# A kernel of cross-attention and sixteen routed experts: sorted places given out two batches at a time, on GpSimd, into tiles left open; two groups of 26 and 6 batches instead of three

## What is computed

```python
# attention: 16 heads of 64, softmax(q k^T + mask) v, then Wo
x = x + xattn(layernorm(x), ctx, ctx, mask, Wq, Wk, Wv, Wo, 16)
# experts: 16 of inner width 128, the 4 best of each token, and one shared by all
scores = sigmoid(xt @ gate_w.T); _, idx = top_k(scores + gate_b, 4)
w = 2.5 * w / sum(w)
for e in range(16): y = y + c_e[:, None] * (silu_and_mul(xt @ w13_e.T) @ w2_e.T)
x = x + y + silu_and_mul(xt @ w13_s.T) @ w2_s.T
```

## Time and profile before

| | us |
|---|---|
| median of 3 runs (lowest, highest) | 2112.61 (2112.27, 2116.42) |
| span of the profiled execution | 2199.6 |
| attention phase in it, to PE's first unit | 1562.3 |
| expert phase in it | 637.3 |

### The profile page before, as it was taken

How to read it: one execution, slowest core, us unless ns; L and a number is a source line. 1 busy time by engine, 2 the same in 40 slices (tenths; PEclk the granted TensorE clock), 3 DMA queues, 4 the chain that set the end, 5 groups by cost and what they waited for, 6 DMA issues and landing times. The chain is left out here.

```text
span 2199.6 us, 57839 instructions
## 1 busy us (share of the span) xinstructions
PE 2073.7 (94%) x16404; PEld 1991.0 (91%) x16404; DVE 1873.9 (85%) x6177; ACT 1681.9 (76%) x4795; POOL 1399.5 (64%) x2094
## 2 busy tenths in 40 slices
PE   7999999999999999999999999999799998898885
PEld 6999999999999998999999998999799898887884
DVE  7999999999999999999999999999864446666687
ACT  6998989889988988988888888889755554454441
POOL 4565655555555555778788877877656646656665
PEclk9999999999999999999999999999999999999997
DMA  7777877778777777866666666666678778888897
GB/s 206 183 184 182 195 182 190 179 179 191 189 185 187 183 171 175 214 181 173 176 179 173 176 168 172 171 173 178 218 263 272 266 244 283 272 285 268 271 335 243
DMA packets 262128, 457.32 MB, mean 208 GB/s; under 512 B 36544, under 2 KB 148672, under 8 KB 261824
## 3 DMA queue, kind: packets, MB, share of 16 engines
q1 hardware_dynamic: 237248, 386.48, 65.4%
q0 software_dynamic: 24576, 67.14, 9.6%
HBM read 141.00 MB, written 144.70 MB: 130 GB/s over the span
## 5 line engine op out<-in xcount | busy, mean ns | idle before, releaser
L812 POOL TENSOR_SCALAR E<-E,rinv 128x256 f32<-128x256 f32 x1024 | 479.6, 479 | 470.3 <-DVE rinv L1136 463.8
L1001 ACT ACTIVATE E<-E,negmax 128x256 f32<-128x256 f32 x1024 | 508.3, 501 | 3.5 <-DVE negmax L1161 3.3
L1161 DVE CUSTOM_DVE_ANT_0 E<-pS,m_in 128x256 f32<-128x256 f32 x1024 | 386.6, 414 | 18.7 <-PE pS L910 16.3
L1180 DVE TENSOR_TENSOR PT_lo<-pT,PT_hi 128x512 fp32r<-128x512 f32 x512 | 350.0, 684 | 23.8 <-ACT PT_hi L1019 20.0
L1636 POOL DMA_INDIRECT block<-expert_rows,slot x256 | 247.6, 967 | 165.9 <-remote 61.4
L1019 ACT ACTIVATE PT_hi<-pT 128x512 fp32r<-128x512 f32 x512 | 304.7, 595 | 9.1 <-PE pT L920 0.5
L920 PE MATMUL pT<-ident,E 128*128 128x128 f32 x2048 | 307.9, 273 | 0.5 <-POOL E L812 0.5
L933 PE MATMUL pV<-PT_hi,V 128*128 128x256 f32 x1024 | 286.1, 301 | 5.3 <-DVE PT_lo L1180 5.3
L909 PE MATMUL pS<-qk_st 128*128 128x256 f32 x1024 | 270.3, 286 | 9.2 <-DMA qk_st<-qk_sp 8.4
L910 PE MATMUL pS<-qk_st,qk_sp 128*128 128x256 f32 x1024 | 266.5, 282 | 0.0
L933 PE MATMUL pV<-PT_lo,V 128*128 128x256 f32 x1024 | 266.2, 282 | 0.0
(11 more groups left out here) (268 smaller groups left out, 6941.0 us busy)
## 6 DMA issues: line engine op xcount, KB each, us to landing
qk_st<-qk_sp SPq DMA_DIRECT2D x512, 192.0 KB
qk_st<-qk_sp SPq DMA_DIRECT2D x512, 128.0 KB
sorted_rows<-qk_st SPq DMA_DIRECT2D x152, 256.0 KB, 3.5
xg<-sorted_rows SPq DMA_DIRECT2D x76, 512.0 KB
expert_rows<-block SPq DMA_DIRECT2D x76, 512.0 KB
acc<-x_plus_attention SPq DMA_DIRECT2D x35, 256.0 KB
x_in<-in_x SPq DMA_DIRECT2D x32, 256.0 KB
c_in<-in_ctxT SPq DMA_DIRECT2D x32, 256.0 KB
```

What stands on the lines that cost most here:

```text
L812: last = pool.tensor_scalar(e[:, t, :], e[:, t, :], rinv[:, r, t:t + 1], 1.0, ALU.mult, ALU.mult)
L1001: last = act.activation(E[r][:, t, :], E[r][:, t, :], ACT.Exp, bias=negmax[:, r, t:t + 1], scale=-1.0, accum_out=rowsum[:, r, t:t + 1])
L1161: last = dve.tensor_tensor_reduce(out=E[r][:, t, :], in0=pS[g % 2][:, t, :], in1=m_in.tile(b)[:, t, :], scale=-1.0, scalar=BIG, op0=ALU.ad ...
L1180: dve.tensor_tensor(lo[:, :, :], pT[n % 2][:, :, :], f32(hi[:, :, :]), ALU.subtract).then_inc(s_ptlo, 1)
```

## The change

Places are given out for each set of two batches instead of for a group, in a running list: an expert whose last tile is not full keeps it open (`room`), and the next set fills it before new tiles are taken, so `units_filled(s)` units are complete after set s. There are two groups, of 26 and 6 batches, with 112 + 32 = 144 sorted units. `ranks` is 5 short matmuls a set. `place` has 23 steps and writes only elementwise instructions (the sums over experts are halvings along the row); in attention POOL runs it, two steps of `place` for each step of attention, for sets 0 to 13; DVE runs it for the last two sets in the expert phase. Scatters follow set by set, one each 1.9 steps from step 87 on: 26 batches in attention, 6 after. The table of experts for each tile (`tabulate`) is made once for each group on DVE. In the expert phase each gather waits only for the units of its own set, gathers begin at unit 34, and 23 dense units stand among the sorted ones; the order is 3 dense, 2 sorted, 1 dense, 28 sorted, then these with four sorted between two, then 26 sorted and 5 dense, 176 in all. Each batch outside the four parked ones uses one accumulator once: 36 loads and 36 stores. Waits are added on SP (a clear of set s waits for those of set s - 2), on DVE (`keep_ranks` and the one-hot of set s wait for the places of set s - 2) and on POOL (the ranks of the set).

```diff
-GROUP_BATCHES = (14, 10, 8)
-EARLY_GROUPS = 2
+GROUP_BATCHES = (26, 6)
 GROUPS = len(GROUP_BATCHES)
 SET_BATCHES = 2
 SETS = GROUP_START[-1] // SET_BATCHES
+GROUP_SETS = [n // SET_BATCHES for n in GROUP_BATCHES]
+FIRST_SET = [start // SET_BATCHES for start in GROUP_START]
+EARLY_SETS = SETS - 2
...
+def units_filled(s):
+
+    rows = (s - FIRST_SET[group_of(s)] + 1) * SET_BATCHES * BATCH_TOKENS * TOPK
+    return ((rows + N_EXPERTS * (P - 1)) // P + 1) // 2
+
+
+PAIRS_OF = [units_filled(FIRST_SET[g + 1] - 1) for g in range(GROUPS)]
+TABLE_COLUMNS = [-(-2 * pairs // P) for pairs in PAIRS_OF]
...
+    RANK_COLUMNS = (SET_TILES + 1) * N_EXPERTS
...
-        for t in range(n - 1):
-            pe.matmul(ps[:, (t + 1) * N_EXPERTS:n * N_EXPERTS].rearrange("p (t e) -> p t e", e=N_EXPERTS),
-                      self.shared.ones[:, :], self.mask[:, at + t, :].unsqueeze(1).broadcast_to([P, n - 1 - t, N_EXPERTS]),
-                      start=False, stop=t == n - 2)
-        for t in range(n):
-            last = pe.matmul(ps[:, n * N_EXPERTS:(n + 1) * N_EXPERTS], self.shared.ones[:, :], self.mask[:, at + t, :],
-                             start=t == 0, stop=t == n - 1)
+        for t in range(SET_TILES):
+            last = pe.matmul(ps[:, (t + 1) * N_EXPERTS:self.RANK_COLUMNS].rearrange("p (t e) -> p t e", e=N_EXPERTS),
+                             self.shared.ones[:, :], self.mask[:, t, :].unsqueeze(1).broadcast_to([P, SET_TILES - t, N_EXPERTS]),
+                             start=False, stop=t == SET_TILES - 1)
...
+    def keep_ranks(self, dve, s, ps):
+        if s >= 2:
+            dve.wait_ge(self.s_slot, s - 1)
+        return dve.tensor_copy(self.pos[s % 2][:, :, :], ps[:, 0:self.RANK_COLUMNS].rearrange("p (t e) -> p t e", e=N_EXPERTS))
+
+    PLACE_STEPS = 23
...
+    def place(self, eng, chain, s, k):
+        opens = s in FIRST_SET
+        rank, count = self.pos[s % 2][:, 0:SET_TILES, :], self.pos[s % 2][:, SET_TILES, :]
...
         if k == 0:
-            self.chain(dve.tensor_scalar(self.over[:, :], self.pos[:, n, :], P / 2 - 0.5, ROUND_TO_TILE, ALU.add, ALU.add))
-            self.chain_here(dve)
-            self.chain(dve.tensor_scalar(self.need[:, :], self.over[:, :], ROUND_TO_TILE, float(P), ALU.subtract, ALU.max))
...
+            if not opens:
+                chain.done(eng.tensor_tensor(self.over[:, :], count, room, ALU.subtract))
+        elif k == 1:
+            chain.done(eng.tensor_scalar(self.over[:, :], count if opens else self.over[:, :], P / 2 - 0.5, ROUND_TO_TILE, ALU.add, ALU.add))
+        elif k == 2:
+            chain.done(eng.tensor_scalar(need, self.over[:, :], ROUND_TO_TILE, float(P) if opens else 0.0, ALU.subtract, ALU.max))
+        elif k == 3:
+            chain.done(eng.tensor_tensor(one, need, shifted(0, 1), ALU.add))
+        elif k == 4:
+            chain.done(eng.tensor_tensor(two, one, shifted(1, 2), ALU.add))
         elif k == 5:
-            ends = self.scan[1]
-            self.chain(dve.tensor_tensor(self.before[:, :], ends[:, :], self.need[:, :], ALU.subtract))
-            self.chain(dve.tensor_scalar(self.done[:, :], ends[:, :], self.shared.tile_at[:, 0:1], None, ALU.is_le))
+            chain.done(eng.tensor_tensor(one, two, shifted(2, 4), ALU.add))
         elif k == 6:
-            self.chain(dve.reduce_sum(self.passed[:, :], self.done[:, :], AXX))
-            self.chain_here(dve)
-            dve.tensor_scalar(self.shared.ended[:, g:g + 1], self.passed[:, :], float(N_EXPERTS - 1), None, ALU.min).then_inc(
-                self.s_ended, 1)
+            chain.done(eng.tensor_tensor(ends if opens else two, one, shifted(1, 8), ALU.add))
+            if not opens:
+                chain.done(eng.tensor_tensor(self.used[:, :], need, room, ALU.add))
         elif k == 7:
-            self.chain(dve.tensor_tensor(self.pos[:, 0:n, :], self.pos[:, 0:n, :],
-                                         self.before[:, :].unsqueeze(1).broadcast_to([P, n, N_EXPERTS]), ALU.add))
+            if not opens:
+                chain.done(eng.tensor_scalar(ends, two, self.ends[:, s - 1, N_EXPERTS - 1:], None, ALU.add))
+        elif k == 8:
+            chain.done(eng.tensor_tensor(fresh, ends, need if opens else self.used[:, :], ALU.subtract))
+        elif k == 9:
+            if not opens:
+                chain.done(eng.tensor_tensor(gap, following, fresh, ALU.subtract))
+                chain.done(eng.tensor_tensor(within, for_tiles(room), rank, ALU.subtract))
+        elif k == 10:
+            chain.done(eng.tensor_tensor(rank, rank, for_tiles(fresh), ALU.add))
+            chain.done(eng.tensor_tensor(room, need if opens else self.used[:, :], count, ALU.subtract))
+            if not opens:
+                chain.done(eng.tensor_scalar(within, within, 0.0, 1.0, ALU.max, ALU.min))
+                chain.done(eng.tensor_scalar(kept, need, 1.0, 1.0, ALU.min, ALU.subtract))
+        elif k == 11:
+            chain.done(eng.tensor_tensor(following, fresh, count, ALU.add))
+            if not opens:
+                chain.done(eng.tensor_tensor(within, within, for_tiles(gap), ALU.mult))
+                chain.done(eng.tensor_tensor(kept, kept, gap, ALU.mult))
+        elif k == 12:
+            if not opens:
+                chain.done(eng.tensor_tensor(rank, rank, within, ALU.add))
+                chain.done(eng.tensor_tensor(following, following, kept, ALU.subtract))
+        elif k == 13:
+            chain.done(eng.tensor_tensor(found[:, :, :, :], self.onehot[s % 2][:, :, :, :],
+                                         rank.unsqueeze(2).broadcast_to([P, SET_TILES, TOPK, N_EXPERTS]), ALU.mult))
+        elif k in (14, 15, 16):
+            half = N_EXPERTS >> (k - 13)
+            chain.done(eng.tensor_tensor(found[:, :, :, 0:half], found[:, :, :, 0:half], found[:, :, :, half:2 * half], ALU.add))
+        elif k == 17:
+            chain.done(eng.tensor_tensor(spot.rearrange("p (t j) -> p t j", j=TOPK), found[:, :, :, 0], found[:, :, :, 1], ALU.add))
+        elif k == 18:
+            chain.done(eng.tensor_scalar(tile, spot, 0.5 - P / 2, ROUND_DOWN_TILE, ALU.add, ALU.add))
+            chain.done(eng.tensor_scalar(quad, spot, 0.5 - QUAD_TILES * P / 2, ROUND_DOWN_QUAD, ALU.add, ALU.add))
+            chain.done(eng.tensor_scalar(four, spot, float(QUAD_TILES), None, ALU.mult))
+        elif k == 19:
+            chain.done(eng.tensor_scalar(tile, tile, ROUND_DOWN_TILE, 1.0 / P - QUAD_TILES, ALU.subtract, ALU.mult))
+            chain.done(eng.tensor_scalar(quad, quad, ROUND_DOWN_QUAD, 1.0 - 1.0 / P, ALU.subtract, ALU.mult))
+        elif k == 20:
+            chain.done(eng.tensor_tensor(four, four, tile, ALU.add))
+        elif k == 21:
+            chain.done(eng.tensor_tensor(four, four, quad, ALU.add))
         else:
...
+            eng.tensor_copy(self.shared.slot[:, SET_TILES * s:SET_TILES * (s + 1), :].rearrange("p t j -> p (t j)"), four).then_inc(
+                self.s_slot, 1)
...
-    RANKS_AT = [(GROUP_START[g + 1] + 2) * H + RANK_STEP for g in range(EARLY_GROUPS)]
+    RANKS_AT = [(SET_BATCHES * s + SET_BATCHES + 2) * H + RANK_STEP for s in range(EARLY_SETS)]
...
+    PLACES = 2
+    place_at = {}
+    for s in range(EARLY_SETS):
+        for k in range(router.PLACE_STEPS):
+            place_at.setdefault(RANKS_AT[s] + 1 + k // PLACES, []).append((s, k))
+
+    SCATTER_STEPS = 1.9
     scatter_at, step = {}, 0.0
-    for b in range(GROUP_START[EARLY_GROUPS]):
-        g = sum(b >= start for start in GROUP_START[1:GROUPS])
-        step = max(step, RANKS_AT[g] + 1 + place_offsets(g)[-1])
+    for b in range(EARLY_SETS * SET_BATCHES):
+        step = max(step, RANKS_AT[b // SET_BATCHES] + 2 + (router.PLACE_STEPS - 1) // PLACES)
...
+    TABLE_AT = RANKS_AT[FIRST_SET[1] - 1] + 4 + (router.PLACE_STEPS - 1) // PLACES
...
+                if s >= 2 and n == units_filled(s) - shared.clears_of(s):
+                    shared.cleared_here(sp, s - 2)
...
+                for s, k in place_at.get(g, ()):
+                    if k == 0:
+                        pool.wait_ge(s_pjfree, number[("rk", s)] + 1)
+                    router.place(pool, router.placing, s, k)
...
+    ENDING = 5
+    waiting = [b for b in range(B) if b not in PARKED]
+    for g in range(GROUPS):
+        for k in range(PAIRS_OF[g]):
+            units.append(("sorted", g, k))
+            while len(waiting) > ENDING and first_c[g] + k + 1 >= sorted_before(waiting[0] // SET_BATCHES) + 4 * (waiting[0] % SET_BATCHES) + 2:
+                units.append(("dense", waiting.pop(0)))
+    units += [("dense", b) for b in waiting]
...
+    LATE_RANKS = {SETS - 2: 0, SETS - 1: CHOOSE_AT + 9}
+    LATE_PLACES = 4
+    LATE_STEPS = -(-router.PLACE_STEPS // LATE_PLACES)
+    TABLE_AT = LATE_RANKS[SETS - 1] + LATE_STEPS + 1
...
+    BATCH_STEPS, SCATTER_FROM = 4, 10
...
+    TILE_STEPS, LAST_STEPS, LANDED = 2.0, 1.2, 7
+    gather_of, gathers_at, from_step = [], {}, float(at)
+    for n in range(B * NT):
```

(12 more changed lines are left out.)

395 lines of the change are left out of this document (174 added, 221 removed).

## The result

In the runs that judged the change, 20 of each kernel on the same chip, the changed kernel took 2112.11 us (2110.15 to 2113.82) and the kernel before 2114.41 us (2112.27 to 2118.52): ratio 0.9986, 95% interval 0.998 to 0.9992, a gain of 2.3 us where 22 were forecast. Its profiled execution has a span of 2112.0 us.

A forecast was written before the change was run, and what follows sets the result against it. PE was taken as attention's bound, DVE close behind; in the expert phase unit transposes set the clock. Attention +31 and expert phase -54 us gave 2177 us profiled, ratio 0.990, so 2091 us, range 2045 to 2140.

The forecast's parts named there:

- dense units out of the queue of gathers: Expert phase: dense units no longer stand in a queue of gathers and fall from 3.30 to 2.57 us each.
- gather units below 3.45 us: Expert phase: sorted units beside gathers fall from 3.45 us to 3.09 us, before contention.
- contention: Expert phase: traffic adds 0.1 us to each of 137 units, +14 us; between nothing and 0.36 us a unit.
- Placing on POOL: Attention: a placement's 34 instructions take 11 us against 8.2 us of room, 2.8 us over for 12 sets, +34 us.
- rival 1: Attention: placing costs no time at a fixed cost of 0.12 us or less; -57 us, 2058 us; chance 0.20.
- rival 2: Attention: POOL becomes the bound through dearer instructions (total zero at 0.26 us fixed); slower, 2148 us; chance 0.22.
- Ranks +6, scatters +4, table +2, leaving -14.8: Attention: 14 sets of rank matmuls, 64 more scatters and the first group's `tabulate` cost these; the two old placements leave.
- Eight units: Expert phase: 8 fewer sorted units make up 25 to 28 us of the -54 us.
- The rest of the expert phase: Beyond the eight units, the -54 us came from dense units at 2.57 us, gather units below 3.45 us, and the end.
- Rival 3: Expert phase keeps its pace of gather units, 3.45 us; +31 - 10 = +21 us, 2133 us; chance 0.13.
- Signs: New trace: PE's POOL waits 25 to 45 us, sorted units near 3.1 us, dense near 2.6, about 35 us after last transposes.
- theory L: From e14's expectation: 35 us gained beyond eight units, from 304 indirect POOL transfers instead of 400, gathers spread over more units.

The follow-up runs named there:

- e9: Changed kernel with the transfers of its expert-phase gathers replaced by fills on POOL, calm condition: 2103.37 us, 0.9935 of the kernel before.
- e3: Changed kernel with eight more sorted units at the end of the first group, stopping condition: 2180.26 us, 0.9914 of the kernel before.
- e4: Changed kernel without computing places in attention for sets 0 to 12 (slots from one iota): 2131.94 us beside 2200.92 of the kernel before, 0.970.
- e6: Changed kernel with placing spread over 23 steps, scatters closer together, first table four steps later: 2138.65 us, 0.9753 of the kernel before.
- e5: Changed kernel run again without edit, stopping condition: 2153.09 us beside 2191.76 of the kernel before.
- e11: Changed kernel without its gathers' transfers (fills on POOL) once more, stopping condition: 2108.19 us, 0.9612 of the kernel before.
- e14: Kernel before with its gathers' transfers replaced by fills on POOL, stopping condition: 2122.67 us beside 2202.87 of the unedited kernel before, 0.9639.
- e1: Kernel before profiled again without edit: span 2200.4 us, and 2200.9 us in nine runs without a profile.
- e12: Changed kernel with stores of the experts' rows cut to 1 KB, gathers reading the sorted rows, stopping condition: 2144.3 us, 0.978 of the kernel before.
- e8: Changed kernel with placing over 16 light steps, no placing or scatter at h = 3, 4, 12, 13; calm: 2100.43 us, 0.9921 of the kernel before.

## Why the prediction was wrong

**The step that failed** is in the sum: "The profiled span is 4.1% over the median of the runs, so I apply the ratio: 2112.6 x 0.990". The trace was of the stopping condition and the runs were of the calm one, and a ratio does not carry over: the 87 us between them lie in the expert phase, at its units beside gathers and scatters. The 3.09, 3.45 and 3.30 us a unit are real, but in the calm condition a unit of the changed kernel takes 2.76 us with or without gathers (e9), and one of the kernel before 2.8 by difference, (552.6 - 38.5) / 184 units. There the terms built on these paces, dense units out of the queue of gathers, gather units below 3.45 us, contention, come to nothing. What is left of -54 us are 8 units, which e3 prices at 19 to 21 us; -21 was measured. That the miss was 20 us and not 33 is luck: attention came out 13 us cheaper than its term.

**The sign that was there** was the difference itself, 2199.6 against 2112.6 us, together with PE's idle time in the class "issue". Two sums should have been made: one with the stops, one with every unit at 2.8 us, where only the 8 units are left, -22 us: +31 - 22 = +9, a forecast of a small loss.

**In the condition of its trace** the expert phase was forecast well, -54 and measured -57, and attention 13 us too dear, +31 and measured +18.2; the ratio was 0.990 and 0.9818. Term by term:

- *Placing on POOL*, +34: 30.0 (e4), 2.5 us a set where 2.8 stood; a placement takes 11.7 us where 11 stood. Part of this is luck. 11.7 us against the room of 8.2 us would have made 3.5 us a set, so either the room is 9.2 us or the mechanism is not this one alone. The second shows in e6: with the room doubled, 13 to 14 of the 30 us go and about 17 stay. Two-input instructions of 16 numbers take 0.213 us (L352) and not 0.23, one-input ones 0.295 (L340). A line through L352 and L378 (256 numbers, 0.679) has an estimated fixed part of 0.18 us; the estimate of 0.11 us that came from the Trainium skill ("GPSIMD Engine Reference", section 3.1) was too low, and rival 1, which needed 0.12, is out. So is rival 2, which needed 0.26.
- *Ranks +6, scatters +4, table +2, leaving -14.8*: e4 has all but the placing, and its first unit stands 11.8 us before that of the kernel before. So the three together cost about 3 us and not 12, if the 14.8 is right; which of them was too dear was not tried.
- *Eight units*, 25 to 28: 19 to 21 (e3).
- *The rest of the expert phase*, -26 to -29 us: -57 + 21 = -36, the stops that go. Calm, it is nothing.
- *Rival 3*, gather units keep their pace: with stops the units take 3.01 us after the change and not 3.45, so no. Calm, gathers slow no unit of the changed kernel (e9), and the rival has no object.
- *Signs*: the waits for POOL were looked for at the transposes alone, 25 to 45 us in all; they are 14.5 us in 8 sets, so some 22 in twelve, more than half of them at the output product. Sorted units near 3.1 us and dense ones near 2.6 were expected from unit 34 on; by the starts of their transposes they take 2.80 and 2.59 us calm, 3.06 and 2.79 with stops. After the last transposes (2074.6 us) 37.4 us follow, where 35 stood.

**Where the expected gain went**, calm: 21 us came from the units, and 18 us were given back in attention: 30 us of placing on POOL against the 12 us that the rest of attention gained.

**The stops.** Shown: they take PE inside chains of products with no wait between (e5). They are there in units beside gathers or scatters and absent where neither runs (e11, e14). Taking 33 MB of gathers away removes 36 of 41 us (e11: 45 less the 9 of the shorter end), taking 37 MB of stores away a fifth (9 of 41 us). So they come with POOL's indirect transfers and not with the total traffic alone; whether with their issue or with their packets was not separated. Their time fits: in e1, 48 of the 68 idle times over 0.3 us of the weight loads in the class "issue", 1640 to 2040 us, begin 0.75 to 1.5 us after POOL started an indirect transfer, where an even spread would give 25; in e5 it is 25 of 38 where 14 would be even, in e12 only 13 of 28 where 11 would.

The changed kernel has 304 such transfers in the expert phase and the kernel before 368, and loses 41 against 77 to 89 us: 0.13 us against 0.21 to 0.24 for each. So theory L's count does not make the difference alone. That the gathers are spread over more units was its other part, and was not tested. What distinguishes the two conditions stays open: one chip showed both, nothing on record says what else ran there, and attention, with 208 scatters of the same kind, shows none.

**The better version** is that of e8: 0.9921 of the kernel before where calm and 0.9762 where stopping, against 0.9986 and 0.9818 of the change as made. Spread evenly (e6) it is the same within the intervals, 0.9753. Of the 30 us of placing about 17 remain, none of it as a wait of PE for POOL; by the traces 6 to 9 of these go with the moved scatters (see e8), the rest is open.

## What to carry to other kernels

When the profiled execution and the runs differ by more than the gain in question, find out first in which phase they differ, and make the sum once for each condition; a ratio over the whole span spreads a local disturbance over terms that it doesn't touch. Work that moves to an idle engine is priced by the room in the steps where it is put, not by the engine's share: the same 34 instructions cost 30 us in 12 steps, about 17 in 16 to 23 with the scatters moved too, and over 60 on the engine that is nearly full.

## What the runs showed of the hardware that was not expected

One program on one chip can run by 4% slower for a whole occasion, at almost the same granted clock (medians of the changed kernel 0.989 calm, 0.987 stopping), with PE idle inside chains of products, for 1.1 us in the row shown under e5, while indirect transfers of POOL's queue are under way. A DVE instruction on 16 numbers took 0.175 us by itself and 0.50 to 0.52 us beside a two-input one of POOL (L295, eight of eight in e6), and a normalization of 256 numbers 0.40 to 0.41 us (e4) against 0.74 to 0.76 us (e6). Small two-input instructions on POOL take 0.21 to 0.23 us for 16 numbers and 0.68 for 256 with a bf16 input (L378), a step of a dependent chain 0.32 us and the cast to integers 0.198 (L397); the clamp with two operations on 64 numbers takes 0.442 (L366).
